# A mixture-of-experts stage that takes two blocks of rows in one slot

## The reference, cut to what matters

```
def _swiglu(x, gu_w, dn_w):
    gate, up = jnp.split(x @ gu_w, 2, axis=-1)
    gate = jnp.clip(gate, -10.0, 10.0)
    return jax.nn.silu(gate) * up @ dn_w
...
for e in range(E):
    out = out + comb[:, e:e + 1] * _swiglu(xn, gate_up_w[e], down_w[e])
```

## Time and profile before

| | us |
|---|---|
| median of three runs | 1613.86 (1612.15 to 1614.66) |
| the profiled execution, its own time | 1616.13 |
| its span in the trace | 1614.4 |
| first X of the stage starts | 700.49 |
| last copy of `psY` in the stage starts | 924.78 |

### The profile page before, as it was taken

How to read it: one execution, slowest core, us unless ns; L and a number is a source line. 1 busy time by engine, 2 the same in 40 slices (tenths; PEclk the granted TensorE clock), 3 DMA queues, 4 the chain that set the end, 5 groups by cost and what they waited for, 6 DMA issues and landing times. The chain is left out here.

```text
span 1614.4 us, 39522 instructions
## 1 busy us (share of the span) xinstructions
PE 1461.4 (91%) x11702; PEld 1106.5 (69%) x11703; DVE 1070.5 (66%) x3467; ACT 1007.1 (62%) x2670; POOL 503.6 (31%) x861
## 2 busy tenths in 40 slices
PE   7999999999999777889999878888888886999998
PEld 5777777777777544568888745555555554777697
DVE  6776777767777466656666537777777763775565
ACT  7887887878878446246666546666666663554454
POOL 4332333323333246033333132332222203552133
PEclk9999999999999997889999979999999997998999
DMA  6000000000000131011111110000000000000000
GB/s 212 2 0 0 0 0 0 0 0 0 0 0 1 37 134 33 34 30 42 42 46 42 33 49 11 13 13 7 13 13 11 9 1 1 2 1 1 1 27 26
DMA packets 34077, 35.77 MB, mean 22 GB/s; under 512 B 5472, under 2 KB 29664, under 8 KB 33120
## 3 DMA queue, kind: packets, MB, share of 16 engines
q1 hardware_dynamic: 29664, 26.08, 5.0%
q0 software_dynamic: 4352, 8.92, 2.2%
HBM read 26.07 MB, written 8.91 MB: 22 GB/s over the span
## 5 line engine op out<-in xcount | busy, mean ns | idle before, releaser
L628 POOL TENSOR_SCALAR a_prob<-a_prob,a_inv 128x128 f32<-128x128 f32 (+1 forms) x256 | 126.4, 504 | 336.6 <-DVE a_inv L516 336.6
L446 ACT ACTIVATE a_prob<-a_psS,a_low 128x128 f32<-128x128 f32 (+1 forms) x512 | 208.9, 427 | 0.9 <-DVE a_low L506 0.9
L1816 ACT ACTIVATE a_probT<-a_psZ 128x512 f32<-128x512 f32 x256 | 139.2, 595 | 90.8 <-PE a_psZ L1602 71.4
L506 DVE CUSTOM_DVE_ANT_0 a_psS<-a_psS,a_bias 128x128 f32<-128x128 f32 (+1 forms) x512 | 167.4, 388 | 42.8 <-PE a_psS L320 38.7
L1899 DVE TENSOR_REDUCE a_low<-a_psS 128x4 f32<-128x1024 f32 x128 | 156.2, 1220 | 53.0 <-remote 34.4
L437 ACT COPY a_probT<-a_psT 128x384 f32<-128x384 f32 x256 | 122.6, 479 | 79.1 <-PE a_psT L366 70.4
L366 PE MATMUL a_psT<-ident,a_prob 128*128 128x128 f32 x768 | 132.8, 282 | 4.9 <-ACT a_probT L437 2.7
L1342 POOL DMA_INDIRECT d_rows<-rows_dram,source x72 | 68.2, 947 | 187.1 <-PE e_psX L1425 135.7
L320 PE MATMUL a_psS<-a_qk 64*128 64x128 f32 (+1 forms) x1024 | 119.6, 352 | 3.4 <-issue 1.6
L366 PEld LDWEIGHTS a_psT<-ident,a_prob 128*128 128x128 f32 x768 | 84.7, 140 | 46.7 <-issue 35.1
L356 PE MATMUL a_psO<-a_probT,a_v 128*64 128x256 f32 (+1 forms) x1024 | 111.5, 339 | 0.6 <-DVE a_o L530 0.6
(11 more groups left out here) (376 smaller groups left out, 4154.1 us busy)
## 6 DMA issues: line engine op xcount, KB each, us to landing
sorted_out<-e_y SPq DMA_DIRECT2D x72, 64.0 KB, 1.5
in_lo<-in_gate_up SPq DMA_DIRECT2D x4, 1024.0 KB, 6.1
x<-in_x SPq DMA_DIRECT2D x8, 256.0 KB, 6.4
down<-in_down SPq DMA_DIRECT2D x1, 2048.0 KB, 15.4
rows_dram<-rows SPq DMA_DIRECT2D x8, 256.0 KB, 2.2
out<-x SPq DMA_DIRECT2D x8, 256.0 KB, 2.3
d_rows<-rows_dram,source POOLq DMA_INDIRECT x72
r_count_wide<-in_count_wide SPq DMA_DIRECT2D x1, 1024.0 KB, 4.7
```

The lines of the kernel that those rows point to most:

```text
L446: nc.scalar.activation(prob[:, 2 * (p % 4) + k, lo:hi], psS[:, u, lo:hi], ACT.Exp, bias=low[:, u, i:i + 1], scale=-1.0, accum_out=total[:, ...
L506: nc.vector.tensor_tensor_reduce(psS[:, u, lo:hi], psS[:, u, lo:hi], bias0[:, 2 * p + k, lo:hi], 1.0, LEAST, ALU.add, ALU.min, low[:, u, i ...
L628: nc.gpsimd.tensor_scalar(w, w, inv[:, 2 * (q % 2) + 1, i:i + 1], 1.0, ALU.mult, ALU.mult).then_inc(norm_done[1], 1)
L1816: nc.scalar.activation(probT[:, (p + half + 1) % 2, 2 * half + c, :, :].rearrange("p j s -> p (j s)"), psZ[:, c, :], ACT.Exp, scale=-1.0). ...
```

## The change

Two blocks make one slot, so there are 36 slots in place of 72. `cols`, `cols_hi`, `cols_lo`, `gate`, `act`, `hidT`, `y` and `psH` become twice as wide. ACT's two passes over the transposed rows, DVE's subtraction, the copy out of `psY` and the store handle both blocks at once. Clip, silu, the product with `psU` and the copy of `psH` stay one instruction per block. `psG` and `psU` keep two buffers, which now hold the two blocks of one slot, so GU of a slot waits until both `hid` of the pair before are written. PE's order in a slot becomes H (eight), X (two), Y (eight products), GU (twelve), with both expert numbers read ahead of Y and both again ahead of GU. ACT's order becomes: both copies of `psH`, silu of the second block of one pair, the two passes over the columns, silu of the first block of the next pair. The core of the diff:

```diff
-        psH = ph.ps("psH", [P, 512])
+        psH = ph.ps("psH", [P, 2, 512])
...
-        N = MOE_BLOCKS
-        dst = g.sorted_out.rearrange("(n p) d -> p n d", p=P)
+        N = MOE_BLOCKS // 2
+        dst = g.sorted_out.rearrange("(n j p) d -> p n j d", p=P, j=2)
...
-            for n in range(2, N):
-                if n >= 4:
-                    pool.wait_ge(turned, n - 3)
-                ring.fetch(n)
+            for i in range(2, 2 * N):
+                if i >= 4:
+                    pool.wait_ge(turned, i // 2 - 1)
+                ring.fetch(i)
...
+            def experts(m):
+                return [pe.value_load(g.expert[0:1, bass.ds(2 * m + k, 1)], min_val=0, max_val=E - 1) for k in range(2)]
+
+            def slot(n, p, r, new, one, two, three):
+                if three:
+                    pe.wait_ge(hid_done, 2 * (n - 2))
+                    pe.wait_ge(h_kept, 2 * (n - 3))
+                    for k in range(2):
+                        for c in range(FC):
+                            mm = pe.transpose(psH[:, k, c * P:(c + 1) * P], hid[:, 2 * ((p + 1) % 2) + k, c * P:(c + 1) * P], g.ident[:])
+                        mm.then_inc(h_turned, 1)
                 if new:
...
+                    if not first_slots(n, 1):
+                        pe.wait_ge(cols_done, n)
+                    for k in range(2):
+                        at = 2 * (p % 2) + k
+                        pe.wait_ge(rows_in[at], r * 32 + 16 * (p // 2) + 16)
+                        mm = pe.transpose(psX[:, k * P:(k + 1) * P], rows[:, at, :], g.ident[:])
+                    mm.then_inc(turned, 1)
+                if three:
+                    e = experts(n - 3)
+                    pe.wait_ge(y_kept, n - 3)
+                    for k in range(2):
+                        pe.wait_ge(h_kept, 2 * (n - 3) + k + 1)
+                        for c in range(FC):
+                            mm = pe.matmul(psY[:, k * D:(k + 1) * D], hidT[:, k, c * P:(c + 1) * P], g.down[:, bass.ds(e[k] * FC + c, 1), :],
+                                           start=(c == 0), stop=(c == FC - 1))
+                    mm.then_inc(y_done, 1)
+                if one:
+                    e = experts(n - 1)
                     pe.wait_ge(lo_done, n)
...
+                    pe.wait_ge(hid_done, 2 * (n - 1))
                     q = (p + 1) % 2
...
+                if three:
+                    act.wait_ge(y_done, n - 3)
+                    for k in range(2):
+                        act.wait_ge(h_turned, 2 * (n - 3) + k + 1)
+                        nc.scalar.copy(hidT[:, k, :], psH[:, k, :]).then_inc(h_kept, 1)
+                if two:
+                    if three:
+                        act.wait_ge(hid_done, 2 * (n - 2))
+                    silu(n - 2, 1)
```

More of the change, by code:

```diff
@@ L1400, in store @@
                     sp.wait_ge(y_kept, r * 2 + k + 1)
-                    sp.dma_start(dst[:, bass.ds(r * 2 + k, 1), :], y_sb[:, k, :]).then_inc(y_out[k], 16)
+                    sp.dma_start(dst[:, bass.ds(r * 2 + k, 1), :, :].rearrange("p n j d -> p (n j) d"), y_sb[:, k, :, :]).then_inc(y_out[k], 16)
                     if k or later:
@@ L1415, in body, with first_slots @@
                 for p in range(4):
-                    slot(r * 4 + p, p, new, has_unit(p, 1), has_unit(p, 2), has_unit(p, 3))
+                    slot(r * 4 + p, p, r, new, has_unit(p, 1), has_unit(p, 2), has_unit(p, 3))
             rounds(eng, body, N // 4)
+        def first_slots(n, count):
+            return isinstance(n, int) and n < count
         @block.tensor
         def _(pe):
-            def slot(n, p, new, one, two, three):
-                if new:
-                    pe.wait_ge(rows_in[p], (n - p) * 4 + 16)
-                    pe.wait_ge(lo_done, n)
[L1425 to L1434, removed]
-                    q = (p + 1) % 2
[L1436 to L1447, removed]
@@ L1452, in _, with silu, slot @@
         def _(act):
-            def slot(n, p, new, one, two, three):
+            def silu(m, k):
+                act.wait_ge(clipped, 2 * m + k + 1)
+                nc.scalar.activation(act_sb[:, k, :], gate[:, k, :], ACT.Silu).then_inc(silu_done, 1)
+            def slot(n, p, r, new, one, two, three):
+                if three:
+                    act.wait_ge(y_done, n - 3)
+                    for k in range(2):
+                        act.wait_ge(h_turned, 2 * (n - 3) + k + 1)
[4 more added lines that the diff above has]
+                    silu(n - 2, 1)
                 if new:
@@ L1456, in slot @@
                     if two:
[L1457 to L1464 removed]
+                        act.wait_ge(in_done, 2 * (n - 1))
+                    nc.scalar.activation(cols_hi[:, p % 2, :], psX[:, 0:2 * P], ACT.Identity, bias=g.affine[:, 1:2], scale=g.affine[:, 0:1])
+                    nc.scalar.activation(cols[:, p % 2, :], psX[:, 0:2 * P], ACT.Identity, bias=g.affine[:, 1:2],
+                                         scale=g.affine[:, 0:1]).then_inc(cols_done, 1)
                 if one:
[L1466 to L1467 removed]
+                    if two:
+                        act.wait_ge(hid_done, 2 * (n - 2) + 1)
+                    silu(n - 1, 0)
             each(act, slot)
@@ L1472, in _, with clip, slot @@
         def _(dve):
-            def slot(n, p, new, one, two, three):
+            def clip(m, k):
+                dve.wait_ge(gate_in, 2 * m + k + 1)
+                nc.vector.tensor_scalar(gate[:, k, :], psG[:, k, :], CLIP, -CLIP, ALU.min, ALU.max).then_inc(clipped, 1)
+            def slot(n, p, r, new, one, two, three):
+                if two:
+                    clip(n - 2, 1)
+                    if not first_slots(n, 4):
+                        dve.wait_ge(h_turned, 2 * (n - 3))
+                    for k in range(2):
+                        dve.wait_ge(silu_done, 2 * (n - 2) + k + 1)
+                        dve.wait_ge(in_done, 2 * (n - 2) + k + 1)
+                        nc.vector.tensor_tensor(hid[:, 2 * (p % 2) + k, :], act_sb[:, k, :], psU[:, k, :], ALU.mult).then_inc(hid_done, 1)
                 if new:
```

50 lines of the change are left out of this document (20 added, 30 removed).

## The result

| | before | after |
|---|---|---|
| median of four runs | 1613.01 (1612.14 to 1614.66) | 1659.16 (1657.67 to 1661.09) |
| span of the profiled execution | 1614.4 | 1659.3 |
| first X of the stage starts | 700.49 | 701.31 |
| last copy of `psY` starts | 924.78 | 968.96 |

The changed kernel is slower: ratio 1.0278, 95% interval 1.0251 to 1.0305, or 46 us. The ratios in this document compare the fast executions of two kernels, each with its 95% interval, and one execution of wait_order_swapped that took 4566.73 us, for a reason that nothing here shows, is left out. The spans differ by 44.9 us. The stage starts 0.8 later, takes 43.4 longer from first X to last copy, and 0.7 more follows behind it.

The account below looks back on a forecast made before the run. The prediction took PE and its instruction stream to bound the stage. A period 1.01 us longer over 34 slots gave 34.3, plus 3.2 fixed: 37.5 on the median of 1613.86, so 1651 us, range 1632 to 1661.

Parts of the forecast that it names:

- The main term: From Y's start to GU: two reads and addresses behind Y's wait take 2.80 us, leaving PE idle 1.02.
- some 0.7: At the stage's start: us added by a second read with its register instructions, half of 1.41, an upper estimate.
- The wait for `hid`: GU's wait for both `hid`: met 3.29 us after H's start (T), before GU's start at T + 4.17, costing nothing.
- Rival A: Ahead of GU: reads cost little, `hid` sets GU's start at T + 3.29; period 6.17, time 1621; chance 9%.
- GU: Twelve gate products in one run take 2.88 us, where two groups of six had 2.96.
- rival B: In GU: the long fp32r run pays, twelve products take 2.56; period 5.85, time 1610.6; chance 4%.
- Reads ahead of Y: Reads between GU and Y: the stream needs at most 3.4 us, 4.0 with the branch, covered by PE's 4.25.
- Rival C: Ahead of Y: stream lead capped at 0.5 us, Y starts at T + 2.07; period 7.75, time 1675; chance 6%.
- H to Y: From H's start to Y's start: 1.37 us, of which PE idles 0.30 waiting for the copy of `psH`.
- The period: One pair of blocks in the stage's middle takes 7.05 us against 6.04, +1.01 over 34 slots.
- The ends: Stage's start and end: first GU near 706.1, last copy out at 961.9; 3.2 us fixed in all.
- The sum: Whole kernel: 37.5 us added, 34.3 recurring and 3.2 fixed, giving 1651; chance 70%.

Follow-up runs that it names:

- wait_order_swapped: Changed kernel with the two waits ahead of Y put back in the old order, `h_kept` before `y_kept`: 1634.11 us, ratio 1.0221 to the kernel before.
- reads_ahead_of_y: Changed kernel with GU's two expert reads moved ahead of Y's wait, beside Y's own two: 1632.74 us, ratio 1.0085 to the kernel before.
- before_read_twice: Kernel before, with GU's expert number read twice in a row in every slot: 1672.3 us, ratio 1.0317.
- copy_silu_copy: Changed kernel with ACT's order first copy of `psH`, silu of the second block, second copy: 1671.07 us, ratio 1.0315 to the kernel before.
- no_reads: Changed kernel with expert numbers read once ahead of the loop, leaving out the choice of expert: 1618.98 us, ratio 0.9988 to the kernel before.
- before_no_reads: Kernel before, with the expert number read once ahead of the loop, leaving out the choice of expert: 1580.36 us, ratio 0.9893.

## Why the prediction was right

1659.16 lies in the range of 1632 to 1661, at its upper end, 8 above the 1651 forecast.

**The start of GU.** The main term was Y to GU at 2.80 and was 2.81 to 2.82. It rested on the stream having nothing queued when Y's wait ends. reads_ahead_of_y moved only the two reads and brought it to 1.78. The 2.80 was chosen near the upper end of the range that I gave, so it is in part luck that it fits to 0.01. So is the "some 0.7" for a read, against 0.71 in before_read_twice: it was half of a stretch with one read and six products, which I had called an upper estimate, and it went into the stage's start alone.

**The wait for `hid`.** I put its end at T + 3.29, below GU's 4.17, so it would not bind. It came at 792.05 - 789.03 = 3.02 and did not bind; copy_silu_copy, with an earlier silu and a later GU, confirms it. The 3.29 was too late by some 0.3, and my expectation for no_reads, which rested on it, missed. Rival A's condition, cheap or overlapping reads, fell with before_read_twice. Where I broke DVE's order, `hid` did bind, so the wait was near.

**GU.** 2.88 forecast, 2.86 measured. The twelve products are 0.23 apart to the end, so rival B falls.

**Reads ahead of Y.** Hidden as forecast. The stream ran further ahead than the 0.5 seen before: two reads, 1.4 by the measured 0.71, fit behind GU. In reads_ahead_of_y four reads, 2.8 in all, fit there in three slots of four, with H to Y at 1.54. The queue of 64 in the Trainium skill (TensorE: Matmul & The Clock Gate, "Architectural detail") agrees. Rival C would have put Y at T + 2.07; it came at T + 1.53. Its sign, "issue" ahead of Y, does stand in the view of waits (0.5 a slot, PEld), but Y's products started with the copy and not later.

**H to Y, the mis-sized term.** "H's start to Y's start is 1.37" was carried over from the stage's end, and was 1.53. The idle time of PE named `hidT` is 0.28 where I said 0.30, but only because X ran longer on PE's record; start to start the miss is 0.16. wait_order_swapped shows 0.10 to 0.11 of it. From the copy's end to Y it was 0.15 in the earlier trace rows, and is 0.26 here (790.56 - 789.72 - 0.58). The prediction has the wait for the copy on a register instruction; in the changed kernel it is on a bare wait ahead of it. I took the number over without seeing that the diff also turns the two waits ahead of Y: the kernel before names `h_kept` first, the changed one `y_kept`. Over 34 slots it is 34 x 0.16 = 5.4 us, nearly all of the 6.2 by which the stage outran its forecast.

**The period.** 7.05 forecast, 7.20 measured: + 0.16 H to Y, + 0.01 to 0.02 Y to GU, - 0.02 GU. PE is busy 85% of the middle where I said some 80%, since its modelled ends run past the starts that follow. The clock stayed full.

**The ends.** GU was to start 5.6 after the first X (706.1 against 700.49) and started 6.3 after it. The fourth block was issued at 703.16, 0.15 later than foreseen beside the stage's later start, and X took it at 705.85, after 2.7. I had used the median landing of 2.2 where one landing sets the time. From that X to the first gate product it took 707.60 - 705.85 = 1.75, where 0.99 with one read and "some 0.7" for the second gave 1.69. From H of the last slot but one to the last copy it took 968.96 - 961.92 = 7.04, where my terms give 6.9. The wider store cost 0.3 more (1.8 against 1.5), as taken.

**The sum.** Inside the stage 37.1 was forecast and 43.4 came: 5.2 from the period, 0.9 up to the first full slot (0.7 of it the late GU), 0.1 at the end. The spans' difference of 44.9 holds another 1.5 us outside the stage. 0.4 of it was in the forecast of 37.5 (the wider store and the wider last copy); the other 1.1 was not, and no run explains it.

## What to carry to other kernels

When work is regrouped, list what the engine's instruction stream has to do between each wait and the next product, not only the products: a value read of 0.71 us is free behind queued work, and costs in full behind a wait; put it ahead of the wait, or put the longest run of products between a result and its use. When one engine's order is turned, turn the order on the engines that serve it in the same edit, or an unmoved copy at the head of a queue becomes the bound.

## What the runs showed of the hardware that I had not expected

- What stands between the wait that ends last and the product costs time after its release: with one instruction less there, Y started 0.10 to 0.11 earlier after its copy (1.53 to 1.43 from H in wait_order_swapped), and with none at all it was another 0.10 (1.33 in no_reads). Where a product waits for two things, it gained here to name the wait that ends last first.
- TensorE's stream ran far enough ahead to hide four reads, 2.8 us by the measured 0.71, behind queued products (reads_ahead_of_y).
- A turn of the loop cost 0.57 on PE where reads follow it, and nothing that can be seen where none do (before_no_reads: 2.82 to 2.83 in each slot). The Trainium skill (Advanced Engine Details and Errata, "Control Flow Timing") gives 51 ns for a branch and 108 ns for compare and branch. So most of the 0.57 is likely the lost lead and the exposed read, not the branch; that wasn't tried apart.
